# Attention heads: row maxima turned once for each head, and copied by VectorE

## The reference, cut to what matters

```
q: 32 heads of 16, k and v: 8 heads of 16, 1024 tokens, rope on q and k
draft  = q k^T                       (causal)
keep   = the 128 largest draft scores of each row
scores = q k^T / 4 where kept, else -inf
out    = softmax(scores) v
```

## Time and profile before

| | us |
|---|---|
| median of three runs | 3204.84 |
| lowest and highest run | 3202.18, 3208.5 |
| profiled execution, from its first to its last instruction (span) | 3199.0 |
| the same execution's time outside the span | not given |

### The profile page before, as it was taken

One profiled execution on the slowest core, in us unless ns is written; L12 is line 12 of the kernel. 1 busy time (PEld: TensorE's weight loads), 2 busy tenths in 40 slices (PEclk: granted clock), 3 DMA queues, 4 the chain that ended last, 5 costly groups with the idle time before them and its releaser, 6 DMA issues. The chain is left out here.

```text
span 3199.0 us, 50581 instructions
## 1 busy us (share of the span) xinstructions
PE 2877.9 (90%) x15823; PEld 1746.2 (55%) x15929; DVE 2459.9 (77%) x4628; ACT 1981.7 (62%) x4218; POOL 1649.3 (52%) x3659
## 2 busy tenths in 40 slices
PE   8899999999999999999999989748887888888779
PEld 4455455454464554554554644526666666666654
DVE  5677687696696786876976976858888888888746
ACT  2464554564564555545645523679999999999823
POOL 3236245264273362452542644777777777777503
PEclk9999999999999999999999999859889988988889
DMA  2222222232132231221321310000000000000010
GB/s 89 66 78 95 73 93 81 71 116 82 66 112 75 74 111 66 89 89 66 104 74 60 119 48 27 2 1 2 2 2 2 2 2 2 2 2 2 1 51 27
DMA packets 65804, 169.63 MB, mean 53 GB/s; under 512 B 11776, under 2 KB 19328, under 8 KB 64512
## 3 DMA queue, kind: packets, MB, share of 16 engines
q1 hardware_dynamic: 54448, 115.17, 11.0%
q10 hardware_dynamic: 11088, 51.19, 4.6%
HBM read 161.08 MB, written 5.24 MB: 52 GB/s over the span
## 5 line engine op out<-in xcount | busy, mean ns | idle before, releaser
L2059 ACT ACTIVATE X<-ah_z,ah_trial 128x256 bf16<-128x256 f32 (+6 forms) x896 | 733.1, 825 | 23.9 <-POOL ah_trial L2162 14.3
L1207 ACT ACTIVATE m_mix<-m_mix,m_cs 128x128 f32<-128x128 f32 x1024 | 312.9, 388 | 254.9 <-DMA m_mix<-cs_rows 254.8
L2012 PE MATMUL ah_ps_o<-a_v,X 128*128 128x17 f32 x2304 | 318.9, 265 | 0.2 <-DVE hT L2270 0.2
L2012 PEld LDWEIGHTS ah_ps_o<-a_v,X 128*128 128x128 f32 x2304 | 303.3, 200 | 0.3 <-issue 0.3
L1089 POOL TENSOR_TENSOR m_xdec<-m_xdt,m_decay_out 128x512 f32<-128x512 f32 x112 | 140.0, 1250 | 213.1 <-DVE m_xdt L1333 202.1
L1117 POOL TENSOR_TENSOR m_squares<-m_squares 128x256 f32<-128x256 f32 x128 | 107.4, 839 | 274.1 <-ACT m_squares L1219 274.1
L2252 DVE MAX8 ah_top<-ah_ps_m 128x8 f32<-128x256 f32 (+6 forms) x224 | 186.0, 830 | 71.4 <-PE ah_ps_m L1962 66.6
L1013 PE MATMUL m_ps_d<-m_w_out,m_gate 128*128 128x512 f32 x512 | 235.2, 602 | 0.0
L1013 PE MATMUL m_ps_x<-m_w_out,m_gate 128*128 128x512 f32 x512 | 233.9, 600 | 0.0
L2070 ACT ACTIVATE X<-ah_ps_e 128x512 f32<-128x512 f32 (+3 forms) x384 | 185.0, 483 | 53.6 <-PE ah_ps_e L1999 44.9
L2231 DVE TENSOR_SCALAR_CACHE_REDUCE X<-ah_z,ah_cut 128x256 bf16<-128x256 f32 (+6 forms) x224 | 193.3, 874 | 26.5 <-POOL ah_cut L2167 26.5
(11 more groups left out here) (319 smaller groups left out, 7556.6 us busy)
## 6 DMA issues: line engine op xcount, KB each, us to landing
m_mix<-cs_rows SPq DMA_DIRECT2D x128, 512.0 KB, 4.3
m_w_proj<-in_w_proj ACTq DMA_DIRECT2D x69, 512.0 KB, 3.3
m_fade<-fade_rows SPq DMA_DIRECT2D x224, 128.0 KB, 2.9
m_w_out<-in_w_out ACTq DMA_DIRECT2D x7, 2048.0 KB, 7.7
X<-in_x SPq DMA_DIRECT2D x8, 256.0 KB, 5.9
m_w_out<-in_w_out SPq DMA_DIRECT2D x1, 2048.0 KB, 10.3
x_away<-X SPq DMA_DIRECT2D x1, 2048.0 KB, 7.3
X<-x_away SPq DMA_DIRECT2D x8, 256.0 KB, 6.2
```

The source lines that it names most:

```text
L1207: act.activation(mix[:, u % 3, h, :], mix[:, u % 3, h, :], ACT.Relu, bias=cs[:, c, h0 + h:h0 + h + 1], scale=-1.0).then_inc(lag_done, 1)
L2012: last = pe.matmul(ps_o[:, t, :], eT[:, g % 3, b * P:(b + 1) * P], v[:, b0 + b, h // REP, :], start=i == 0 and b == 0, stop=b0 + b == t, s ...
L2059: act.activation(sign[:, at % 2, 0:(t + 1) * P], z[:, h % RING, cols(t)], ACT.Sign, bias=trial[:, h % RING, 0, t - 1:t], scale=-1.0, accum ...
```

## The change

The eight tiles' parts are packed into 32 columns of one 128x128 block (`parts_all`, four columns for each tile). TensorE turns it with one matmul at t = 2, into 128 columns of `ps_x`; the second turning at t = 7 is gone. VectorE, not ScalarE, copies the turned block (128x128 to bf16) to `rows`, right behind its third pick; `rows` now has two buffers, by head. `minus_rows` becomes eight stationary blocks, one for each tile, that pick the tile's four rows out of the common block; VectorE builds them after the loop's first step (`row_factors`), and the big clearing of `parts` and the three fills of `minus_rows` before the loop are gone or smaller.

```diff
@@ tables and tensors
-    ROWS_BEFORE = {14: 0, len(SWEEPS) * W: 1}
-        rows = sb("rows", [P, S], BF16)
+        rows = sb("rows", [P, 2, P], BF16)
+        row_weight = sb("row_weight", [P, NT, 4])
+        row_factor = sb("row_factor", [P, NT])
-        minus_rows = sb("minus_rows", [P, P], BF16)
+        minus_rows = sb("minus_rows", [P, NT, P], BF16)
+        parts_all = sb("parts", [P, P], BF16)
+        parts = parts_all[:, 0:4 * NT].rearrange("p (t j) -> p t j", t=NT)
-        parts = spare[:, 7 * BANK:8 * BANK].bitcast(BF16).rearrange("p (t q) -> p t q", t=NT)
+        ps_rows = ps_x[:, P:2 * P]
-        SET_UP = 11
+        SET_UP = 8
+        FACTORS = SET_UP + 5
@@ TensorE: sample
-                    pe.wait_ge(rows_done, 2 * (h - 3))
+                    pe.wait_ge(rows_done, h - 3)
@@ TensorE
-            def turned_rows(h, half):
+            def turned_rows(h):
                 pe.wait_ge(split_done, h + 1)
-                if half == 0 and h + 3 < AH:
+                if h + 3 < AH:
                     pe.wait_ge(stats_done, 3 * (h + 4))
-                elif half or h:
-                    pe.wait_ge(rows_done, 2 * h + half)
-                for t in range(4):
-                    last = pe.matmul(ps_x[:, t * P:(t + 1) * P], parts[:, 4 * half + t, :], env.ident_bf[:],
-                                     start=t == 0, stop=True, skip_group_check=True)
-                last.then_inc(row_done, 1)
+                if h:
+                    pe.wait_ge(rows_done, h)
+                pe.matmul(ps_rows, parts_all[:], env.ident_bf[:], start=True, stop=True).then_inc(row_done, 1)
@@ TensorE: exponents
-                pe.wait_ge(rows_done, 2 * h + 1 + t // 4)
+                pe.wait_ge(rows_done, h + 1)
+                if g == 0:
+                    pe.wait_ge(set_up, FACTORS)
-                pe.matmul(out[:, 0:w, :], minus_rows[:], rows[:, t * P:(t + 1) * P].unsqueeze(1).to_broadcast([P, w, P]),
+                pe.matmul(out[:, 0:w, :], minus_rows[:, t, :], rows[:, h % 2].unsqueeze(1).to_broadcast([P, w, P]),
@@ TensorE: the loop
-                    if live(n - 2) and t in (2, 7):
-                        turned_rows(n - 2, t // 7)
+                    if live(n - 2) and t == 2:
+                        turned_rows(n - 2)
@@ ScalarE
-            def row_out(h, half):
-                act.wait_ge(row_done, 2 * h + half + 1)
-                if h:
-                    act.wait_ge(et_done, (h - 1) * NCH + LAST_CHUNK[3 if half == 0 else 7] + 1)
-                act.activation(rows[:, half * BANK:(half + 1) * BANK], ps_x[:], ACT.Copy).then_inc(rows_done, 1)
-                        if live(n - 2) and at in ROWS_BEFORE:
-                            row_out(n - 2, ROWS_BEFORE[at])
-                if live(n - 2):
-                    row_out(n - 2, ROWS_BEFORE[at])
@@ VectorE
+            def row_out(h):
+                dve.wait_ge(row_done, h + 1)
+                if h >= 2:
+                    dve.wait_ge(et_done, (h - 1) * NCH)
+                dve.tensor_copy(rows[:, h % 2], ps_rows).then_inc(rows_done, 1)
-            dve.memset(parts, 0.0).then_inc(set_up, 1)
-            dve.memset(minus_rows[:], 0.0).then_inc(set_up, 1)
+            dve.memset(parts_all[:], 0.0).then_inc(set_up, 1)
-            dve.memset(minus_rows[0:4, :], -BIG).then_inc(set_up, 1)
-            dve.wait_ge(set_up, SET_UP - 1)
-            dve.memset(minus_rows[0:3, :], -1.0).then_inc(set_up, 1)
+            def row_factors():
+                dve.memset(row_weight[:, :, 0:3], -1.0).then_inc(set_up, 1)
+                dve.memset(row_weight[:, :, 3], -BIG).then_inc(set_up, 1)
+                dve.wait_ge(set_up, SET_UP + 2)
+                dve.tensor_tensor(row_weight[:], row_weight[:], env.ident[:, 0:4 * NT].rearrange("p (t j) -> p t j", t=NT),
+                                  ALU.mult).then_inc(set_up, 1)
+                dve.wait_ge(set_up, SET_UP + 3)
+                dve.tensor_reduce(row_factor[:], row_weight[:], AX.X, ALU.add).then_inc(set_up, 1)
+                dve.wait_ge(set_up, SET_UP + 4)
+                dve.tensor_copy(minus_rows[:], row_factor[:].unsqueeze(2).to_broadcast([P, NT, P])).then_inc(set_up, 1)
@@ VectorE: the loop
                         pick(n - 2, t)
+                        if t == 3:
+                            row_out(n - 2)
...
+                if n == FIRST:
+                    row_factors()
```

More of the change, by code:

```diff
@@ L2174, in split_max @@
                 if h:
-                    pool.wait_ge(row_done, 2 * h)
+                    pool.wait_ge(row_done, h)
                 pool.tensor_copy(parts[:, :, 0], row_max[:, h % 4]).then_inc(own, 1)
@@ L2276, in _ @@
             dve.memset(far[:, 1], FAR).then_inc(set_up, 1)
-            dve.memset(parts, 0.0).then_inc(set_up, 1)
-            dve.memset(minus_rows[:], 0.0).then_inc(set_up, 1)
+            dve.memset(parts_all[:], 0.0).then_inc(set_up, 1)
             dve.tensor_scalar(ident_taken[:], env.ident_bf[:], TAKEN, None, ALU.mult).then_inc(set_up, 1)
             dve.tensor_scalar(ident_back[:], env.ident_bf[:], BIG / TAKEN, None, ALU.mult).then_inc(set_up, 1)
-            dve.wait_ge(set_up, 8)
+            dve.wait_ge(set_up, SET_UP - 1)
             dve.memset(parts[:, 1:NT, 3], 1.0).then_inc(set_up, 1)
-            dve.memset(minus_rows[0:4, :], -BIG).then_inc(set_up, 1)
-            dve.wait_ge(set_up, SET_UP - 1)
-            dve.memset(minus_rows[0:3, :], -1.0).then_inc(set_up, 1)
+            def row_factors():
[8 more added lines that the diff above has]
+                dve.tensor_copy(minus_rows[:], row_factor[:].unsqueeze(2).to_broadcast([P, NT, P])).then_inc(set_up, 1)
             dve.wait_ge(table_in, 32)
```

## The result

| | median us | lowest to highest | runs |
|---|---|---|---|
| before | 3203.64 | 3202.0 to 3208.5 | 20 |
| changed | 3207.78 | 3205.21 to 3212.19 | 20 |

The changed kernel takes 1.0014 times as long as the one before (95% interval 1.0007 to 1.0020); the medians are 4.1 us apart. That is a small loss, clear of zero and within the 0.2% that the forecast counted as no change (forecast 3207.1 us).

What follows compares the result with a forecast made beforehand. The prediction took VectorE and TensorE in turn, not ScalarE, to set the pace. Copy with turning +1.4, `row_factors` +1.4, drain -1.5 and clock +1.0 gave +2.3 on 3204.84: 3207.1 us, range 3200 to 3213, chance 0.51.

Steps and rivals of the forecast that it cites:

- ScalarE's copies at 0: Two ScalarE row copies go, 0.98 us a head; no gain in the 24 heads, only more waiting at the exponentials.
- VectorE's copy at +0.21: The 128x128 copy behind VectorE's third pick lies on the path and adds 0.21 us a head.
- the copy is dear: Rival: VectorE's copy takes 0.42 us, twice its row, so the loop grows by 6.7 us to 3214 us; chance 0.11.
- Turning at t = 2 at -0.165: Three of TensorE's four matmuls there go, on the path to the third pick, saving 0.165 us a head.
- the prediction's own sign: Test in the changed profile: a 24-head mean off 29.6 us by more than 0.1 makes the clock's part wrong.
- Turning at t = 7, and the gap: Four TensorE matmuls, 0.22 us, go at no gain; the wait behind them grows from 1.06 to 1.28 us.
- `row_factors` at +1.4: On VectorE between first and second step, 1.9 us long; delays the chain to the first cut by 1.4 us.
- The drain at -1.5: In the last three heads VectorE waits for the cut; one saved ScalarE copy each, 3 x 0.49, gives -1.5 us.
- The clock at +1: TensorE's wider gap pushes its clock slightly to the slow side; the pattern of heads most likely holds, +1 us.
- The rival built on the wider gap, +9 us: Rival: TensorE idles longer ahead of tile 0's scores, its lower clock comes sooner; +9 us, 3215 us; chance 0.20.
- the first step: The part on ScalarE's two row copies that go, taken at 0 because nobody waits for ScalarE there.
- the clock falls the good way: Rival: all heads start like the short one of 29.03 us; 15 us less, 3192 us; chance 0.12.

Runs made afterwards that it cites:

- e1: The changed kernel plus two idle ScalarE copies of 128x512 per step, on spare memory, where the row copies stood; 3203.54 us, 1.0002 against the kernel before.
- e2: The changed kernel with the one 128x128 copy made by ScalarE, ahead of its 15th count, and none by VectorE; 3199.77 us, 0.9988 against the kernel before.
- e3: The changed kernel with a second 128x128 copy on VectorE, into a spare buffer nobody reads; 3216.89 us, 1.0042 against the kernel before.
- e5: The changed kernel with `row_factors` called ahead of the loop, before VectorE's wait for the table's DMA; 3206.12 us, 1.0010 against the kernel before.
- e4: The changed kernel with four unread matmuls of 128 columns put back at t = 7; 3206.79 us, 1.0008 against the kernel before.
- e12: The changed kernel with `row_factors` ahead of the loop and four and three unread 512-column matmuls in TensorE's two gaps; 3174.27 us, 0.9907 against the kernel before.
- e7: The changed kernel with three unread 512-column matmuls ahead of the first marked scores alone; 3194.0 us, 0.9969 against the kernel before.

## Why the prediction was right, and where it was not

The forecast was 3207.1 us, no change beyond 0.2%, with its own range from 3200 to 3213. The median is 3207.78. That the two agree within 0.7 us is in part luck: the base of the sum, 3204.84 us from three runs, is 1.2 us above the median of twenty (3203.64), while the sum, +2.3 us, is 1.8 below the 4.1 that were measured. Step by step:

- *ScalarE's copies at 0.* Right, and shown: e1 gives the work back and loses nothing. The waits at the exponentials went to 48.1 us (some 45 foretold).
- *VectorE's copy at +0.21.* Right: +0.20 from start to start, +0.23 in the segment's mean. e2 and e3 show that it is on the path; at 0.28 us long, and 0.20 from start to start, the rival "the copy is dear" (0.42) falls.
- *Turning at t = 2 at -0.165.* Not settled. First take to third pick fell by 0.08 us in the mean in the profile of the changed kernel, by 0.21 in that of e5, whose heads are the same code, and by 0.18 in e1. One profile of the kernel before stands against them, and two executions differ by nearly as much as the term. The same holds for the head as a whole: it grew by 0.16 us in changed and by 0.04 in e5, where the sum had 0.045. By the prediction's own sign (a mean more than 0.1 us off 29.6 makes the clock's part wrong) 29.73 would count against it and e5's 29.62 for it: the sign is finer than what one profile can tell.
- *Turning at t = 7, and the gap.* Right: 1.29 us (1.28 foretold). The wait covers the work: with it put back in e4 the kernel is no slower.
- *`row_factors` at +1.4.* Direction and path right, size half: +0.76. The copy to 128x1024 took 0.69 us, not 1.1, and the function 1.2 us, not 1.9. e5 moves it behind a DMA's wait and the 0.76 us are gone.
- *The drain at -1.5.* Wrong sign in the one execution, +2.1 us, but -1.1 in e5, which runs the same code there. What speaks against the mechanism is that the waits for the cut, which were to shrink by the saved copies, grew from 4.5 us to 5.9 (6.0 in e5). The stretch took 123.0 us before, 125.1 in changed, 121.9 in e5, 123.6 in e1, 126.2 in e2 and e4, and 130.4 in e3. No mechanism was found for this scatter; it stays open, and so does a term of a microsecond or two here.
- *The clock at +1.* Not told apart from 0 by any run. The 24 heads have the same mean clock (0.90), and putting the gap back (e4) moved the median by 1.0 us, less than its interval. The rival built on the wider gap, +9 us, falls with both. What the clock does is more indirect: e2 moved the time by -8.0 us where the copy's price is 6.4 (0.20 x 32), e3 by +9.1. In e2 ten of 24 heads are under 29.35 us, in changed seven, in e3 none (before: eight). So a step of 0.2 us also shifts how heads fall against the slow stretches. That reading rests on counts in single executions, and it is not shown.

One sentence under the first step, "Nobody waits for ScalarE here", says too much. The longest entry in the list of waits of the kernel before is GpSimd's wait for the count, 127.0 us in the 24 heads:

```profile
POOL ah_trial L2132 <- ACT X L2059: 127.0, 66, 2.8
```

What holds is the other half of the argument: GpSimd's cut was in time, so no engine on the path waited for ScalarE.

So the mechanism was as foretold: the copy moved onto the path, the work taken off ScalarE bought nothing. The medians differ by some 4 us where the sum had 2.3. The one term that the traces show to be mis-sized is `row_factors` (0.6 us too high); the drain's -1.5 us is not seen, and its waits moved the other way. The 1 to 3 us that are left lie in the heads or the drain, and single profiles don't resolve them. The rival "the clock falls the good way" (3192 us) was not this change's outcome. Its price was that of heads all like the short one, at a clock of 0.92; e12, where matmuls that nobody reads keep the clock at 0.99, takes 3174 us.

## What to carry to other kernels

Before work is moved off the fullest engine, read the list of waits: if that engine waits for another, and no engine on the path waits for it or for what hangs on it, the work it gives up becomes waiting, and an engine on the path that takes the work over pays for it. Where TensorE's granted clock stays under 1.0 in a loop with gaps of about a microsecond, as here (0.90), a few matmuls that nobody reads, put into those gaps, are a cheap trial; look afterwards for the bound that comes next (here probably the count and move loop between ScalarE and GpSimd). And take a second profile of the same kernel before a difference of 0.1 us a head is given a cause.

## What the runs showed of the hardware that was not expected

- Two gaps of TensorE of 1.0 to 1.3 us in each head of 29.6 us go with a mean granted clock of 0.90. The slow part lies behind the gaps: 0.67 from first take to third pick, 1.00 from there to the next row maximum, 0.85 to the next take. Three matmuls of 512 columns in the first gap raised the mean to 0.96, four and three in both to 0.99; three in the second gap alone left it at 0.91 and moved the slow stretch (e7). Four matmuls of 128 columns at t = 7, which narrowed the gap from 1.29 to 1.05 us, left it at 0.90 (e4).
- TensorE's busy time fell while more matmuls ran at the higher clock: 576.84 us in changed, 562.47 in e12 with seven more of 512 columns in each head. A TensorE busier by the profile is not one that does more.
- VectorE's copy of a value broadcast along the free axis, 128x1024 to bf16, took 0.69 us; a cast of 128x512 from SBUF, half as many elements, took 0.56.
